# A state-space stage with its residual on TensorE: identity matmuls, 64x64 projections on a swapped copy, and a stage without loops

## The reference, cut to what matters

```python
xz = einsum('bld,ed->ble', x, W_in); xs, z = split(xz, 2)
xs = silu(conv4(xs) + conv_b)                       # causal, 4 taps, per channel
dt, Bm, Cm = split(einsum('bld,ed->ble', xs, W_xproj), [4, 6])   # 4 + 2 + 2 columns
dt = softplus(dt @ W_dt.T + b_dt)
h  = exp(dt * A) * h + dt * Bm * xs                 # the scan, 2 states per channel
y  = (sum_n h_n * C_n + xs * D) * silu(z)
y  = layernorm(y @ W_out.T) * ln_g + ln_b           # over the 64 output channels
x  = x + y                                          # the residual
```

## Time and profile before

| | |
|---|---|
| profiled execution: device time / span | 667.71 us / 665.6 us |
| TensorE busy over the span | 610.3 us (92%) |
| VectorE busy | 520.9 us (78%) |
| GpSimd busy | 396.2 us (60%) |
| ScalarE busy | 387.0 us (58%) |
| mean granted TensorE clock | 0.987 |
| state-space turns | about 69 to 203 us of the span |

### The profile page before, as it was taken

The page is one execution under the profiler, slowest core; times in us unless marked ns, Lnnn a source line. Parts: engine busy times, 40 slices in busy tenths (PEclk is TensorE's granted clock), DMA queues, the critical chain, the costliest instruction groups (busy, mean ns, idle before and its releaser), DMA issues.

```text
span 665.6 us, 8799 instructions
## 1 busy us (share of the span) xinstructions
PE 610.3 (92%) x2926; PEld 259.5 (39%) x2926; DVE 520.9 (78%) x840; ACT 387.0 (58%) x696; POOL 396.2 (60%) x251
## 2 busy tenths in 40 slices
PE   7888688888788999999999999999999999999987
PEld 5436233332245333233444434334443344432324
DVE  7996889999983347888868878698887988866662
ACT  3478289999854533306468485584755846657400
POOL 3464477878831214011995959759598495898710
PEclk9998799999989999999999999999999999999989
DMA  8800000000002548340403004040040400003663
GB/s 331 283 2 1 0 0 0 0 0 0 0 2 62 136 109 198 88 96 0 96 1 88 8 4 91 0 96 0 34 96 0 110 20 34 0 35 113 211 219 122
DMA packets 19798, 44.74 MB, mean 67 GB/s; under 512 B 5160, under 2 KB 5288, under 8 KB 19632
## 3 DMA queue, kind: packets, MB, share of 16 engines
q1 hardware_dynamic: 17040, 35.11, 18.2%
q10 hardware_dynamic: 1440, 4.55, 2.8%
q0 software_dynamic: 1280, 4.60, 2.4%
HBM read 10.42 MB, written 13.02 MB: 35 GB/s over the span
## 4 chain that ended last, share of the span: by engine, by line
PE 55%; DVE 27%; issue 8%; ACT 5%; POOL 3%; DMA 1%; DVEq 0%; POOLq 0%; ACTq 0%
PE PS L1806 14%; PE PS L1793 10%; PE PS L1771 7%; PE PS L1679 6%; DVE SM L766 5%; DVE RB L523 4%; PE PS L1760 3%; PE PS L1938 3%; PE PS L1688 2%; DVE RB L599 2%; DVE PS L591 2%; DVE RB L606 1%; DVE SM L502 1%; DVE RB L795 1%; PE PS L1558 1%
## 5 line engine op out<-in xcount | busy, mean ns | idle before, releaser
L766 DVE TENSOR_REDUCE SM<-PS 128x1 f32<-128x512 f32 x256 | 164.2, 683 | 46.8 <-PE PS L1771 46.3
L1203 ACT ACTIVATE RB<-PS 128x512 f32<-128x512 f32 x256 | 138.9, 595 | 88.3 <-PE PS L1793 86.0
L1452 POOL TENSOR_TENSOR RB<-RB 128x1024 f32<-128x1024 f32 x60 | 141.5, 2378 | 15.6 <-DVE RB L909 10.0
L1793 PE MATMUL PS<-R 98*128 98x512 f32 x256 | 96.1, 452 | 5.7 <-ACT RB L1203 5.6
L1771 PE MATMUL PS<-R 96*128 96x512 f32 x256 | 86.6, 411 | 4.5 <-DVE SM L766 3.9
L1806 PE MATMUL PS<-RB 128*64 128x512 f32 x320 | 85.6, 616 | 0.3 <-ACT RA L1219 0.2
L1793 PEld LDWEIGHTS PS<-R 98*128 98x128 f32 x256 | 39.4, 188 | 86.5 <-ACT RB L1203 52.2
L1602 PE MATMUL PS<-RA,W 128*128 (+1 forms) x128 | 63.0, 637 | 6.7 <-DVE RB L599 6.5
L1771 PEld LDWEIGHTS PS<-R 96*128 96x128 f32 x256 | 47.7, 189 | 33.2 <-DVE SM L766 20.6
L1452 POOL TENSOR_TENSOR EX<-EX,RB 128x1024 f32<-128x1024 f32 x24 | 56.4, 2370 | 2.1 <-issue 1.2
L1806 PE MATMUL PS<-RB,RA 128*64 128x512 f32 x192 | 51.8, 618 | 0.2 <-ACT RA L1219 0.2
(11 more groups left out here) (212 smaller groups left out, 1031.7 us busy)
## 6 DMA issues: line engine op xcount, KB each, us to landing
R<-WS SPq DMA_DIRECT2D x72, 128.0 KB, 2.4
planes<-R SPq DMA_DIRECT2D x8, 528.0 KB
X<-x SPq DMA_DIRECT2D x8, 512.0 KB, 8.4
RB<-RB SPq DMA_DIRECT2D x32, 128.0 KB, 4.1
RB<-RB ACTq DMA_DIRECT2D x14, 280.5 KB, 3.7
out<-X SPq DMA_DIRECT2D x7, 512.0 KB, 4.2
planes<-RA SPq DMA_DIRECT2D x6, 544.5 KB, 2.9
R<-R SPq DMA_DIRECT2D x20, 128.0 KB, 2.5
```

The source lines that it names most:

```text
L766: v.tensor_reduce(MX[:, par, tile, h:h + 1], bank(2 + h), AX.X, ALU.max)\
L1203: act(slot[:, h * HALF:(h + 1) * HALF], bank(4 + h), ACT.Exp).then_inc(s["p_ready"], 1)
L1452: i = g.tensor_tensor(out, out, PT[j % SLOTS][par], ALU.add)
L1793: mm(bank(4 + h), stack(b, par, 1)[0:98, j * P:(j + 1) * P], stack(b, par, 0)[0:98, h * HALF:(h + 1) * HALF]).then_inc(s["t_mm"], 1)
```

## The change

VectorE loses `residual0`; its `norm` now also multiplies by ln_g and writes to SBUF (`tQ`). TensorE adds x and that product in bank 0 with two matmuls by the identity (`residual`), and ScalarE reads bank 0 twice (`copy0`, `square0`). B and C are each four 64x64 matmuls, two of which read a copy of xs with its halves of partitions swapped (`XT`), which 16 new DMAs on SP's queue make. `soft` and `soft_log` use bank 7 instead of bank 0. The hardware loops of the stage become written-out turns on four engines. The core of the diff:

```diff
+        XT = [R[:, (3 + p) * L:(4 + p) * L].bitcast(F32) for p in range(6)] + [WS[:, i, :].bitcast(F32) for i in range(2)]
+        def growth(p):
+            return bank(7 if p else 0)
...
+            for p in range(PAIRS):
+                sp.wait_ge(s["silux_done"], p + 1)
+                sp.dma_start(XT[p][OF_A, :], XS[OF_B, p, :]).then_inc(swapped[p], 16)
+                sp.dma_start(XT[p][OF_B, :], XS[OF_A, p, :]).then_inc(swapped[p], 16)
...
             def norm(p, h):
                 n = 2 * p + h
                 v.wait_ge(s["r_done"], n + 1)
-                v.tensor_tensor(product(p, h), product(p, h), tR[h], ALU.mult).then_inc(s["normed0"], 1)
-            def residual0(p, h):
-                n = 2 * p + h
-                v.wait_ge(s["normed0"], n + 1)
-                v.scalar_tensor_tensor(half(X, p, h), product(p, h), col("lng"), half(X, p, h), ALU.mult, ALU.add)\
-                    .then_inc(s["blk0_done"], 1)
+                v.scalar_tensor_tensor(tQ[h], product(p, h), col("lng"), tR[h], ALU.mult, ALU.mult)\
+                    .then_inc(s["normed0"], 1)
...
-            with v.Fori(1, PAIRS - 1) as p:
+            for p in range(1, PAIRS - 1):
                 turn(p, 0)
                 turn(p, 1)
...
-            v.tensor_tensor(MV, XSUM[:, :, 0, :], XSUM[:, :, 1, :], ALU.add).then_inc(s["stat_ready"], 1)
+            link(v.tensor_tensor(MV, XSUM[:, :, 0, :], XSUM[:, :, 1, :], ALU.add))
+            v.tensor_scalar(MV, MV, 1.0 / L, None, ALU.mult).then_inc(s["stat_ready"], 1)
...
-            def sums0(p, h):
...
+            def copy0(p, h):
+                a.wait_ge(s["res_mm"], 2 * p + h + 1)
+                act(half(X, p, h), bank(0), ACT.Copy, accum_out=XSUM[:, p, h, 0:1]).then_inc(s["x0_done"], 1)
+            def square0(p, h):
+                act(half(ZS, p, h), bank(0), ACT.Square, accum_out=XSUM[:, p, h, 1:2])\
+                    .then_inc(s["sums_done"], 1)
             def turn(p, h, lead=True, lag=True):
+                if p > 0:
+                    copy0(p - 1, h)
                 if lag:
                     square(*before(p, h))
+                if p > 0:
+                    square0(p - 1, h)
                 if lead:
                     soft_parts(p + 1, h)
                     soft(p + 1, h)
...
-                if not isinstance(p, int) or p > 0:
-                    sums0(p - 1, h)
...
             def dt(p, h):
                 n = 2 * p + h
-                need(t, s["dt_read"], n)
+                if p < 1 or (p, h) == (1, 0):
+                    need(t, s["dt_read"], n)
+                else:
+                    t.wait_ge(s["nd_done"], n)
+                    t.wait_ge(s["ln_done"], n)
                 mm(bank(7), WDT[:, :], half(XS, p, h)).then_inc(s["dt_mm"], 1)
             def states(p, h, o):
...
-                for j in range(STATE):
-                    i = mm(bank(1 + 2 * o + j), mat("bc%d" % (2 * o + j)), half(XS, p, h))
+                if h == 0 and o == 0:
+                    t.wait_ge(swapped[p], 32)
+                for j, rows in enumerate((OF_A, OF_B)):
+                    for image in range(2):
+                        src = half(XS, p, h) if image == j else XT[p][:, h * HALF:(h + 1) * HALF]
+                        i = mm(PS[image * C:(image + 1) * C, 1 + 2 * o + j, :],
+                               mat("bc%d" % (2 * o + j))[rows, j * C:(j + 1) * C], src[rows, :])
             def project_out(p, h):
                 n = 2 * p + h
-                if isinstance(p, int) and (p, h) == (PAIRS - 1, 1):
+                if (p, h) == (PAIRS - 1, 1):
                     t.wait_ge(s["y_last"], 1)
-                    t.wait_ge(s["dt_read"], 2 * PAIRS)
                 else:
                     t.wait_ge(s["y_done"], n + 1)
-                    need(t, s["blk0_done"], n)
+                need(t, s["normed0"], n)
                 mm(product(p, h), mat("wout"), tY[h]).then_inc(s["o_mm"], 1)
+            def residual(p, h):
+                n = 2 * p + h
...
+                need(t, s["sums_done"], n)
+                mm(bank(0), mat("ident"), half(X, p, h), start=True, stop=False)
+                t.wait_ge(s["normed0"], n + 1)
+                mm(bank(0), mat("ident"), tQ[h], start=False, stop=True).then_inc(s["res_mm"], 1)
             def turn(p, h, lead=True, lag=True):
+                if p > 0:
+                    residual(p - 1, h)
                 if lead:
                     dt(p + 1, h)
                 if lag:
                     project_out(*before(p, h))
...
-            t.wait_ge(s["nd_done"], 2 * PAIRS)
-            t.wait_ge(s["ln_done"], 2 * PAIRS)
+            t.wait_ge(s["scan_done"], 2 * PAIRS)
             idle(32)
             project_out(PAIRS - 1, 1)
             idle(8)
+            residual(PAIRS - 1, 0)
             variance(PAIRS - 1, 1)
-            idle(72)
+            idle(40)
+            residual(PAIRS - 1, 1)
+            idle(36)
             group(GN1)
```

More of the change, by code:

```diff
@@ L83, in link @@
         ins.then_inc(self.sem, 1)
[L84 to L94, removed]
+        self.eng.wait_ge(self.sem, self.k)
 def need(eng, sem, value):
@@ L280, in product @@
         def product(p, h):
-            return bank(7 if isinstance(p, int) and (p, h) == (PAIRS - 1, 1) else 5)
+            return bank(5)
+        def growth(p):
+            return bank(7 if p else 0)
         SLOTS1 = 9
@@ L333, in build @@
             g_ready xb_done xz_mm tap_done taps_done silux_done siluz_done
-            dt_mm b_mm c_mm o_mm v_mm e_done dta_read u_done dt_read nd_done ln_done dt_done dtx_done
-            b_read da_done scan_done c_read hc_done y_done y_last sq_done r_done normed0 blk0_done sums_done
+            res_mm dt_mm b_mm c_mm o_mm v_mm e_done dta_read u_done dt_read nd_done ln_done dt_done dtx_done
+            b_read da_done scan_done c_read hc_done y_done y_last sq_done r_done normed0 x0_done sums_done
             g1_ready ua_done ub_first ub_done shifted_even shifted_odd moved_even moved_odd conv_mm y1_done w1_mm x1_done
@@ L343, in build @@
         gathered = [ctx.enter_context(nc.semaphore("gathered%d" % p)) for p in range(PAIRS)]
+        swapped = [ctx.enter_context(nc.semaphore("swapped%d" % p)) for p in range(PAIRS)]
         x_in = [ctx.enter_context(nc.semaphore("x_in%d" % p)) for p in range(PAIRS)]
@@ L500, in stats @@
             def stats(p, h):
[L501 to L503 removed]
+                return v.bn_stats(BST[:, p, h, :], half(X, p, h))
             def input_stats(p):
@@ L582, in soft @@
                 v.wait_ge(s["u_done"], n + 1)
-                v.scalar_tensor_tensor(tE[h], bank(0), -1.0, tE[h], ALU.add, ALU.subtract)\
+                v.scalar_tensor_tensor(tE[h], growth(p), -1.0, tE[h], ALU.add, ALU.subtract)\
                     .then_inc(s["nd_done"], 1)
@@ L643, in turn @@
                     norm(*before(p, h))
-                    residual0(*before(p, h))
             def shifts():
@@ L1016, in soft @@
                 need(a, s["ln_done"], n)
-                act(bank(0), tE[h], ACT.Identity, bias=ONE).then_inc(s["u_done"], 1)
+                a.wait_ge(s["dt_read"], n + 1)
+                act(growth(p), tE[h], ACT.Identity, bias=ONE).then_inc(s["u_done"], 1)
             first(0, 0)
@@ L1021, in _ @@
             second(0, 0)
-            with a.Fori(1, PAIRS // 2) as k:
+            for k in range(1, PAIRS // 2):
                 first(2 * k, 0)
@@ L1038, in soft_log @@
                 need(a, s["b_read"], n - 1)
-                act(tU[h], bank(0), ACT.Ln).then_inc(s["ln_done"], 1)
+                act(tU[h], growth(p), ACT.Ln).then_inc(s["ln_done"], 1)
             def grow(p, h):
@@ L1104, in _ @@
             turn(1, 1)
-            with a.Fori(2, PAIRS - 1) as p:
-                ch.enter(p - 2, 2)
+            for p in range(2, PAIRS - 1):
                 turn(p, 0)
                 turn(p, 1)
-                ch.leave(PAIRS - 3)
             turn(PAIRS - 1, 0, lead=False)
@@ L1113, in _ @@
             inverse_sd(PAIRS - 1, 1)
-            sums0(PAIRS - 1, 0)
-            sums0(PAIRS - 1, 1)
+            for h in range(2):
+                copy0(PAIRS - 1, h)
+                square0(PAIRS - 1, h)
             root(GN1)
@@ L1400, in _ @@
             output(1, 0)
-            with g.Fori(2, PAIRS) as p:
-                ch.enter(p - 2, 4)
+            for p in range(2, PAIRS):
                 soft(p, 0)
@@ L1644, in _ @@
             turn(0, 1)
-            with t.Fori(1, PAIRS - 1) as p:
+            for p in range(1, PAIRS - 1):
                 turn(p, 0)
```

29 lines of the change are left out of this document (9 added, 20 removed).

## The result

The kernel after takes 677.46 us (median; 676.36 to 683.66), beside 668.26 us (667.01 to 669.13) for the kernel before on the same chip: a ratio of 1.0173, 95% interval 1.0143 to 1.0202. It is slower, as forecast (676.7 us, 671 to 685). The profiled execution took 678.17 us, its span is 676.3 us, so 10.7 us more than before.

The account below looks back on a forecast made before the run. VectorE bounds the stage at 7.89 us per half turn; after the change a loop through TensorE and ScalarE would, at 8.58. First turns -2.4, steps +8.3 and -0.7, tail +3.8: +9.0 on 667.71, so 676.7 us, range 671 to 685.

Parts of the forecast that it names:

- The loop: Steady half turns: norm, residual, dt, projection, ScalarE's list, next norm take 8.58 us against 7.89; twelve steps cost +8.3 us.
- dt's wait: TensorE, steady half turn: dt's new wait for ln_done ends 1.70 us after r_done, costing nothing, 0.09 to spare.
- The comparison with the loop of before: Old loop 7.11 us; the change takes 0.82, adds 1.73 of matmuls and 0.61 of ScalarE, less 0.10.
- rival C: Steady half turns: TensorE's clock falls in longer gaps, 2.9 us of loop matmuls double; 708 us in all; 10%.
- The pulled-ahead weights: Projection's weight load on TensorE: streaming saves 0.10 us; the skill's early-load rule would lower the sum 1.2 us, not taken.
- The first turns: Start of the stage: half the states passes end 3.2 us sooner; gain 1.5 to 3.2 us, 2.4 taken.
- Step fourteen to fifteen: Second-last step of the stage, bound by VectorE: 7.35 us loses the old residual instruction L622, -0.7 us.
- The tail: Behind the last step, all in series: projection +0.65, variance +1.34, statistics +1.83; together +3.8 us.
- The swap DMAs and the code: SP's queue and instruction fetches: swaps of 2.1 us cost nothing, or some 4 us if late; fetches 0 to 1.3, none taken.
- Loop instructions gone: nothing: Steady half turn: removing the hardware loop instructions gains nothing, as they don't stand in this loop.
- A: Steady half turns: dt and projection overtake the waiting residual, ScalarE's 7.12 us sets the pace; 659.2 us; 12%.
- B: Steady half turns: only dt gets out of the loop, 7.72 us per half turn; 666.4 us; 6%.

Follow-up runs that it names:

- dt_behind: Changed kernel with the dt matmul behind the output projection in TensorE's list instead of ahead of it; 665.85 us, ratio 0.9997 to the kernel before.
- dt_twice: Changed kernel with each dt matmul issued twice from the second pair on, same result; 688.86 us in one run.
- c_twice: Changed kernel with C's four 64x64 matmuls issued twice for pairs 2 to 7, same result; 678.32 us in one run.
- full_states: Changed kernel with B and C again as two 128x128 matmuls each and no swap DMAs; 678.8 us in one run.
- growth_sbuf: Changed kernel with 1 + e in SBUF instead of bank 7 from pair 2 on, and dt ahead of the residual on TensorE; 673.01 us, ratio 1.0112.
- before_quads: before_written_out plus B and C as four 64x64 matmuls each, XT and the 16 swap DMAs, residual0 left on VectorE; 663.91 us, ratio 0.9943.
- before_written_out: Kernel before with only this stage's hardware loops replaced by written-out turns; 667.79 us, ratio 1.0009.
- all_behind: reorder with 1 + e back in bank 7 and TensorE's order projection, dt, variance, residual; 666.36 us, ratio 0.9989.
- reorder: growth_sbuf plus residual behind projection, copy0 and square0 ending ScalarE's turn, last projection in bank 7, last variance ahead of residual of 14; 667.7 us, ratio 1.0005.
- norm_later: all_behind with norm of n-2 moved on VectorE from the end of turn n-1 to behind inputs of turn n; 669.74 us, ratio 1.0040.
- states_first: norm_later with TensorE's residual of n-2 moved behind states of n+1; 663.84 us, ratio 0.9959.

## Why the prediction was right

**The loop** was there as drawn, hand-over by hand-over, as far as dt. Where the prediction summed 0.04 + 0.75 + 0.04 + 0.96 + 0.86 + 1.06 + 4.26 + 0.61, after shows 0.04 from `r_done` to `norm`, 0.80 to the residual, 1.01 to dt, 0.93 to the projection, 1.06 to `square` and 4.84 to the next `r_done`. Undoing one part (dt_behind) and doubling one (dt_twice) moved the pitch by what the loop says; c_twice and full_states, the same engine off the loop, moved it by nothing.

What releases dt in the end, though, is not the residual but dt's own wait. In every steady half turn its weights load 0.12 us after `ln_done` (129.45 after 129.33), exactly as in growth_sbuf, where nothing stood ahead of them (84.74 after 84.05 + 0.57 = 84.62). So a second loop sets the 8.68: `r_done` to `ln_done` 1.70, to dt 0.15, to the projection 0.93, to `square` 1.06, to the next `r_done` 4.84, in all 8.68, without `norm` and the residual. The forecast loop runs just behind it: the 7.70 that dt_behind leaves, and dt's 0.86, make 8.56. Both go through dt and the projection, so the runs above act on both. Taking only the residual out of dt's way would by this estimate have gained nothing; no run did that. That the two loops are within 0.12 us of each other is chance, and the forecast number owes something to it.

**The mis-sized term** is dt's wait: "it costs nothing, with 0.09 to spare". `ln_done` came at 129.33, 1.70 after `r_done`, as forecast, and before the residual had passed. But dt's weights could not be loaded ahead: they were loaded at 129.45, with the matmul, as those of a matmul behind a wait, 0.12 after `ln_done` where 0.04 was taken for a hand-over. dt then started 1.01 after the residual instead of 0.96, and the projection 0.93 after dt instead of 0.86. To cost nothing, the wait has to be over in time for the weights to load under the matmul ahead, as in dt_behind (131.23, 0.29 before the projection itself). This is 0.12 of a half turn, less 0.03 that ScalarE's list came shorter: 8.68 for 8.58, and with it the 1.2 us by which the twelve steps missed.

Two sums beside the forecast are off without touching it. The comparison with the loop of before, 0.82 less and 1.73 more, gives 8.53; by the listed terms it is 0.86 less and 1.82 more. And rival C has 2.9 us of matmuls double, but prices it at 2.6. Of the signs, TensorE's idle time ahead of the residual's second matmul was 0.97 where 1.5 was named.

**The pulled-ahead weights.** In dt_behind the projection's weights were loaded while the residual ran, in after dt's were not. So the rule that the prediction weighed (the Trainium skill, TensorE: Matmul & The Clock Gate, The mechanism) holds here for a matmul whose wait is over while the one ahead still runs, and the row was right for one that has to wait longer.

**The first turns** gained 3.1 where 2.4 was taken of 1.5 to 3.2. full_states puts 1.3 of that, and 0.6 in the next step, on the quads; before_quads, with L622 still there, gains 2.4. The rest was not separated. **Step fourteen to fifteen** gained 1.1 for 0.7; before_written_out alone gains 0.4 there (6.94 for 7.35), which was not in the term. **The tail** was right at 3.9 for 3.8. The trace shows L613 of 15 at 208.92, after 5.74 us of waiting for `inverse_sd`, and beside and behind it `copy0` and `square0` of 14, the residual of 15 and its `copy0` and `square0` in series.

**The swap DMAs and the code** cost nothing that the trace shows. From the DMA view of after:

```profile
q8 instruction: 25, 0.41, 0.3%
...
R<-RA SPq DMA_DIRECT2D x12, 256.0 KB, 3.7
```

A swap took 3.7 us where 2.1 was taken from the earlier trace rows, and no idle time of `states` ends with one. The instruction queue moved 0.05 MB more; whether the +0.4 us behind the stage is from that stays open.

**"Loop instructions gone: nothing"** was right for after, whose pace is the loop, and wrong for VectorE's own pace: before_written_out runs at 7.67 instead of 7.89. Measured against that, the loop costs 12 x (8.68 - 7.67) = 12.1 us.

**Rivals.** A (TensorE lets dt and the projection overtake) didn't happen: L1588 and L1610 follow L1621 in every half turn. Its pace, ScalarE's 7.12, was out of reach too as the orders stood: all_behind, with nothing left behind the wait, ran at 7.53. B's arithmetic (7.72, 666.4 us) is what dt_behind measured (7.70, 665.85 us). C did not appear in the steady half turns of after: the granted clock is 1.00 from 80 to 200 us, with TensorE idle 0.97 before the residual. It did appear in single steps of growth_sbuf, reorder and all_behind.

## What to carry to other kernels

When an operation moves from a full engine to one that has time, count the ring that it closes, not the busy share: follow the wait that it brings through everything queued behind it, back to what it waits for. Work that is ready should stand ahead of a wait in an in-order list, not behind; exchanging two matmuls was worth 11.6 us here (677.46 and 665.85). Where two waits end close together at one instruction, look for a second loop before clearing the first. And each such move has to be walked again, since norm_later opened one ring and closed another.

## What was not expected of the hardware

In these traces VectorE and GpSimd lengthened each other's instructions where VectorE's reads came from SBUF: L579 0.69 to 1.53 and L1380 1.27 to 1.78 in growth_sbuf, `skip` 0.75 to 1.35 in states_first. The Trainium skill says so (SBUF — State Buffer, SBUF: two separate sides): an instruction of VectorE with two SBUF inputs and one of GpSimd that reads SBUF exclude each other, and the one that starts first keeps the other out until it is done. The traces agree in both orders, with the numbers above, but not to the end: the VectorE instruction that came second was done some 0.55 us after GpSimd's, less than its own 0.69 to 0.75. The collision may be what keeps states_first at 7.43, since its `skip` is 0.4 to 0.6 us longer in each half turn; that is an estimate, as a kernel with open rings and without the collision was not tried.

Writing the loops out made VectorE's own instructions follow each other sooner, 0.21 us in a half turn of eight instructions, without one instruction becoming faster: the two steps that shrank are from `outputs` to `skip` (1.37 to 1.26) and from `norm` to `residual0` (0.86 and 0.81 in turns to 0.73).
